# One step of a routing computation moved from slot five to slot six on VectorE, in a linear-attention and mixture-of-experts kernel

## The chip, the cores and the metric

The kernel runs on 1 core of one Trainium2 chip, as one launch. The metric is the device time of the launch in microseconds (us), median of several runs. TensorE's granted clock was 0.999 of full speed in the profiled execution.

## The reference

`x` has 4 sequences of 2048 tokens of 256 numbers. The output is `x + attention(xn) + experts(xn)`, where `xn` is the layer norm of `x` over its last axis.

- Attention: 8 heads with keys of 128 and values of 64. `q`, `k`, `v` are products of `xn` with weights, `alpha = sigmoid((xn @ Wg + bg) / 16)` is a decay for each token and head. A state per head follows `state = alpha * state + k v^T` from token to token, and a token's output is `q` times the state. The outputs are multiplied by `sigmoid(xn @ Wog)` and by `Wo`.
- Experts: `scores = sigmoid(xn @ gate_w^T)` over 64 experts in 8 groups of 8, plus a bias. A group's score is the sum of its two highest entries. The four best groups are kept, and among their experts the eight best. Their scores, brought to a sum of 2.5, are the weights. Each expert takes its tokens in order up to 256, and applies `silu(x w_gate) * (x w_up)` and `w_down`. The results are added to their tokens with the weights.

```python
sfc = scores + gate_bias[None, :]
group_scores = jax.lax.top_k(sfc.reshape(n, G, E // G), 2)[0].sum(-1)
gidx = jax.lax.top_k(group_scores, TG)[1]
```

## The kernel before

**Tiles and steps.** The tokens are cut into 16 tiles, each of 128 tokens of each of the four sequences (512 tokens in all). The attention goes through the tiles in 16 steps, one tile a step, since each needs the state that the one before left. A step has a slot 0 and slots 1 to 8 (`s`), one for each head, and each slot has up to five places (`place`) at which other work is put "beside" the attention (the functions `beside`). The order of every engine's program is written out by hand: an engine works through its instructions in the order of its own `step` function, and waits on semaphores (`wait_ge`) for the others. There is no planner.

**What is beside the attention.** In the early steps (kind "norm", steps 0 to 4) each step normalises and routes three more tiles: first, second and third tile of the step, which are `3c+1`, `3c+2` and `3c+3` for step `c`. Step 5 ("count") and step 6 ("slots") make the lists of the experts' tokens, steps 7 to 14 run eight experts each, and step 15 is the last. On VectorE steps 1 to 3 are a hardware loop, and steps 0 and 4 are written out.

**Routing one tile on VectorE** has five parts, each a chain of small instructions:
- `gates` (L1333) adds the bias to the decay's input; `decays_products` (L1339, L1341, L1344) makes the running products of the decays.
- `route_groups` (L1351 to L1364), thirteen instructions: the biased scores, and for each group the sum of its two highest, into `gsc`. It needs ScalarE's `score` (L1093).
- `route_ranks` (L1372 to L1378): the groups' ranks, from `gsc`.
- `route_top` (L1385 to L1392): the eight best experts.
- `route_weights` (L1401 to L1406): their weights. GpSimd then stores them.

For the second tile of a step: TensorE makes the logits in slot 4 (L723), ScalarE `score` in slot 4, VectorE the group scores at the head of slot 5 and ranks and best experts at the end of slot 6, and the weights in slot 7. `statistics` (L1315 to L1320) and `scales` (L1326, L1327) of the third tile are in slot 6, with ScalarE's square root (L1071) between them and its `normalise` (L1078) behind them.

**The attention on VectorE.** At the start of slot `s` VectorE multiplies the scores of head `s-1`, which TensorE made in bank 2 (L847), by the decays, into `At` (L1533). TensorE's scores of the next head wait until that has read the bank. Then comes a decay scan of a later head (L1512). In odd slots VectorE scales the queries of a pair of heads into `carry` (L1545): ScalarE's copy of the queries in slots 2, 4 and 6 (L1142) of the same step waits for one of those scalings. In even slots TensorE makes the update (L879) and the outputs of the pair (L865, L868), which need both `At` of the pair. VectorE then gates the outputs (`pair_gated`, L1555) and brings the state up (`pair_state`, L1569 and L1572; in step 0 a copy, L1564). ScalarE copies the update (L1156), TensorE transposes it back (L891), and L1572 or L1564 needs that. Then ScalarE's high part of the gated outputs (L1160) and VectorE's low part (L1576, `outs_low`). In slot 8 VectorE also makes the low part of the next tile's tokens (L1416), for which TensorE waits at the start of its next step (L810). Queries and keys are projected at L795.

**VectorE's order in slots 5 and 6** of an early step before the change is: `At`, ends, scan, `route_groups` of the second tile, `decays_products` of the second tile, queries scaled; `At`, `statistics`, scan, `scales`, `pair_gated`, `pair_state`, `route_ranks` and `route_top` of the second tile, `outs_low`.

Of the kernel before, what the change touches and what calls it, by code (L numbers as in the profile page):

```python
# [77 lines left out]
def build(nc, x_in, Wq, Wk, Wv, Wo, Wg, bg, Wog, gate_w, gate_bias, w_gate, w_up, w_down, out):  # L78
    with ExitStack() as ctx:
# [236 lines left out]
        def is_first(c):  # L316
            return isinstance(c, int) and c == 0
# [975 lines left out]
        def _(dve):  # L1293
            tt, ts = dve.tensor_tensor, dve.tensor_scalar

            def chained(semaphore, base):

                n = [0]

                def link(ins, apart=False):  # L1300
                    n[0] += 1
                    ins.then_inc(semaphore, 1)
                    if apart:
                        wait_apart(dve, semaphore, base + n[0])
                    else:
                        dve.wait_ge(semaphore, base + n[0])
                return link, n
# [14 lines left out]
            def scales(c):  # L1322
                link, n = chained(norm_chain, c * NORM_CHAIN + 2)
                dve.wait_ge(std_ready, c + 1)
                wait_past(dve, xn_ready, c)
                link(dve.reciprocal(rstd, std))  # L1326
                dve.scalar_tensor_tensor(shift, mv[:, :, 0], -1.0, rstd, ALU.mult, ALU.mult).then_inc(rstd_ready, 1)  # L1327
# [18 lines left out]
            def route_groups(c):  # L1346

                link, n = chained(route_chain, c * ROUTE_CHAIN)
                dve.wait_ge(score_ready, c + 1)
                sfc_t = sfc.rearrange("p a b -> p (a b)").rearrange("p (b e) -> p b e", b=B)  # L1350
                link(tt(sfc_t, score, bias_e[:, None, :].broadcast_to([P, B, E]), ALU.add))  # L1351

                tt(hi1, sfc[:, :, 0:4], sfc[:, :, 4:8], ALU.max)
                link(tt(lo1, sfc[:, :, 0:4], sfc[:, :, 4:8], ALU.min))
                tt(mid, hi1[:, :, 0:2], hi1[:, :, 2:4], ALU.min)
                tt(hi2, hi1[:, :, 0:2], hi1[:, :, 2:4], ALU.max)
                link(tt(lo2, lo1[:, :, 0:2], lo1[:, :, 2:4], ALU.max))
                link(tt(lo2, lo2, mid, ALU.max))
                tt(mid[:, :, 0:1], hi2[:, :, 0:1], hi2[:, :, 1:2], ALU.min)
                tt(hi3, hi2[:, :, 0:1], hi2[:, :, 1:2], ALU.max)  # L1360
                link(tt(lo3, lo2[:, :, 0:1], lo2[:, :, 1:2], ALU.max))
                link(tt(lo3, lo3, mid[:, :, 0:1], ALU.max))
                gsum = gsc.rearrange("p b g -> p (b g)")
                link(tt(gsum[:, :, None], hi3, lo3, ALU.add), apart=True)  # L1364
                assert n[0] == ROUTE_LINKS[0]

            def route_ranks(c):

                link, n = chained(route_chain, c * ROUTE_CHAIN + sum(ROUTE_LINKS[:1]))
                left_out = rank.rearrange("p (b g) -> p b g", b=B)  # L1370
                for b in range(B):
                    ins = dve.max(top8[:, b, :], gsc[:, b, :])  # L1372
                link(ins, apart=True)
                link(dve.memset(top8[:, :, TG:K], BIG), apart=True)
                for b in range(B):
                    ins = dve.match_replace(left_out[:, b, :], top8[:, b, :], gsc[:, b, :], -TAKEN)
                link(ins)
                link(tt(left_out, left_out, gsc, ALU.is_equal))  # L1378
                assert n[0] == ROUTE_LINKS[1]

            def route_top(c):

                link, n = chained(route_chain, c * ROUTE_CHAIN + sum(ROUTE_LINKS[:2]))
                masked_g = masked.rearrange("p b e -> p (b e)").rearrange("p (a g) -> p a g", g=EG)
                ins = dve.scalar_tensor_tensor(masked_g, rank[:, :, None].broadcast_to([P, B * G, EG]), -BIG, sfc,  # L1385
                                               ALU.mult, ALU.add)
                link(ins, apart=True)
                for b in range(B):
                    ins = dve.max(top8[:, b, :], masked[:, b, :])
                link(ins, apart=True)  # L1390
                for b in range(B):
                    ins = dve.match_replace(left[:, b, :], top8[:, b, :], masked[:, b, :], -TAKEN)  # L1392
                link(ins)
                assert n[0] == ROUTE_LINKS[2]

            def route_weights(c):

                link, n = chained(route_chain, c * ROUTE_CHAIN + sum(ROUTE_LINKS[:3]))
                wait_past(dve, sel_kept, c)
                wait_past(dve, wt_stored, 16 * c)  # L1400
                link(tt(chosen, left, masked, ALU.not_equal))  # L1401
                link(tt(weight, score, chosen, ALU.mult))
                link(dve.tensor_reduce(total, weight, AX.X, ALU.add))
                link(ts(total, total, 1e-20, None, ALU.add))
                link(dve.reciprocal(inv, total))
                dve.scalar_tensor_tensor(weight, weight, SCALE_OUT, inv[:, :, None].broadcast_to([P, B, E]),  # L1406
                                         ALU.mult, ALU.mult).then_inc(weight_ready, 1)
                assert n[0] == ROUTE_LINKS[3]
# [223 lines left out]
            def beside(c, kind, s, place):  # L1632


                if kind == "norm":
                    n = STEP_N * c + 1 + s // 3
                    if s == 0 and place == 3:
                        if not is_first(c):
                            route_groups(n - 1)
                            scales(n)  # L1640
                    if s in (3, 6) and place == 1:
                        scales(n)
                    if (s, place) in ((0, 4), (3, 3), (6, 3)):
                        route_ranks(n - 1)
                        route_top(n - 1)
                    if s % 3 == 1 and place == 1:
                        route_weights(n - 1)
                    if (s, place) in ((1, 3), (4, 3), (H, 1)):
                        gates(n)
                    if s in (2, 5) and place == 0:  # L1650
                        route_groups(n)
                    if (s, place) in ((2, 1), (5, 1), (H, 3)):
                        decays_products(n)
                    if s in (2, H) and place == 3 and not (isinstance(n, int) and n == C - 1):
                        statistics(n + 1)
                if kind == "count" and s == 0 and place == 3:
                    route_groups(C - 1)
                    route_ranks(C - 1)
                if kind == "count" and s == 0 and place == 4:
                    route_top(C - 1)  # L1660
                    route_weights(C - 1)
                if kind == "count" and s > 0:
                    for pe_place in {2: (1, 2), 3: (3,)}.get(place, ()):
                        if (s, pe_place) in COUNT_AT:
                            keep_group(COUNT_AT.index((s, pe_place)))
                    if place == 3 and s == H:
                        keep_totals()
                if kind == "slots" and s == 0 and place == 1:
                    keep_firsts()
                if kind == "slots" and (s, place) in FOUR_AT:  # L1670
                    count_four(FOUR_AT.index((s, place)))
                if kind == "slots" and s == H and place == 3:
                    make_lists()
                if kind == "experts" and s > 0:
                    if place == 0:
                        if s > 1:
                            tokens_low_e(c, s - 1)
                        if s == H:
                            hidden_low(c, s - 2)
                            down_low(c, s - 2)  # L1680
                    if place == 1 and 1 < s < H:
                        expert_out(c, s - 2)
                    if place == 2 and s < H:
                        expert_hidden(c, s - 1)
                        weights_low_e(c, s)
                        if s < H - 1:
                            hidden_low(c, s - 1)
                            down_low(c, s - 1)
                    if place == 4 and s == H:
                        expert_hidden(c, s - 1)  # L1690
                        expert_out(c, s - 2)
# [107 lines left out]
```

## Time and profile before

| what | value |
|---|---|
| median of 3 runs | 1258.42 us (1258.26 to 1258.51) |
| the profiled execution | 1258.32 us, span 1256.7 us |
| TensorE busy over the span | 1233.2 us (98%) |
| VectorE | 976.3 us (78%) |
| ScalarE | 624.1 us (50%) |
| GpSimd | 483.9 us (39%) |
| chain that ended last | PE 83%, DVE 11%, issue 3%, ACT 2%, DMA 1% |

The profile is of one execution. "Busy" is the time in which an engine has an instruction in work, and the chain is followed back from the last instruction to whatever released each. PE is TensorE, PEld its weight loads, DVE VectorE, ACT ScalarE, POOL GpSimd. Times in the timelines are us from the start of the span. The projections of the values that begin the early steps (L810) start at 14.1, 87.5, 162.2, 236.6 and 311.0 us, and those of the step behind them at 384.9.

### The profile page before, as it was taken

The page shows a single profiled execution, that of the slowest core. Times are in us where ns is not written, and L with a number is a line of the kernel's source. Part 1 is how long each engine was busy: PE and PEld are TensorE (multiplying, and loading weights), DVE is VectorE, ACT ScalarE, POOL GpSimd, SP SyncE. Part 2 cuts the span into 40 slices and gives each one's busy share as a digit, 9 for nine tenths or more (in the row PEclk, how much of TensorE's full clock was granted, in tenths as well). Part 3 has the DMA queues.
Part 4 walks back from the last instruction along what each step waited for, and adds up shares of the span by engine and source line. Part 5 has one row for each costly group of instructions (what it writes and reads, how often), then busy time and mean ns, then how long its engine had stood idle before and what let it go on. Part 6 is the DMA issues. An engine that isn't in the chain of part 4 may idle for free.

```text
span 1256.7 us, 28686 instructions
## 1 busy us (share of the span) xinstructions
PE 1233.2 (98%) x9922; PEld 1092.0 (87%) x9922; DVE 976.3 (78%) x2343; ACT 624.1 (50%) x1319; POOL 483.9 (39%) x377
## 2 busy tenths in 40 slices
PE   7899999999999999999999999999999999999998
PEld 6788888888888888899999999998999999989987
DVE  6997878889797579778688587786885877868834
ACT  6675756666574544444444344444443444444432
POOL 2110011001101035238457365484574754745720
PEclk9999999999999999999999999999999999999999
DMA  6576534355342313258487476584875766747765
GB/s 241 169 239 217 179 120 159 123 173 173 117 165 77 102 68 102 86 144 195 108 186 180 124 176 150 139 192 109 196 166 125 169 157 143 188 108 193 170 188 181
DMA packets 124920, 194.68 MB, mean 155 GB/s; under 512 B 12016, under 2 KB 98608, under 8 KB 124592
## 3 DMA queue, kind: packets, MB, share of 16 engines
q1 hardware_dynamic: 94384, 147.99, 36.7%
q0 software_dynamic: 30464, 45.83, 20.0%
q8 instruction: 34, 0.56, 0.2%
q14 instruction: 38, 0.31, 0.1%
HBM read 148.62 MB, written 57.74 MB: 164 GB/s over the span
## 4 chain that ended last, share of the span: by engine, by line
PE 83%; DVE 11%; issue 3%; ACT 2%; DMA 1%; DVEq 0%; SPq 0%; ACTq 0%
PE bank L795 24%; PE bank L939 7%; PE bank L847 7%; PE bank L810 7%; PE bank L907 7%; PE bank L827 6%; PE bank L879 4%; PE bank L865 4%; PE bank L950 4%; PE bank L868 4%; PE bank L838 3%; PE bank L891 2%; PE bank L929 2%; DVE Dt L1512 2%; DVE At L1533 1%
## 5 line engine op out<-in xcount | busy, mean ns | idle before, releaser
L635 POOL DMA_INDIRECT acc<-arena,idx_all x128 | 220.2, 1720 | 146.2 <-DMA acc<-res 53.5
L627 POOL DMA_INDIRECT arena<-table,idx_all x132 | 166.6, 1262 | 157.0 <-ACT share L1166 95.7
L795 PE MATMUL bank<-xp,wq 128*128 128x512 f32 x768 | 209.2, 408 | 0.0
L795 PE MATMUL bank<-xp,wk 128*128 128x512 f32 x768 | 202.1, 398 | 0.0
L795 PEld LDWEIGHTS bank<-xp,wk 128*128 128x128 f32 x768 | 138.5, 188 | 29.0
L795 PEld LDWEIGHTS bank<-xp,wq 128*128 128x128 f32 x768 | 137.0, 190 | 25.2 <-issue 0.5
L1512 DVE TENSOR_TENSOR_SCAN Dt<-decay,eye_b 128x512 f32<-128x512 f32 x128 | 157.4, 1231 | 0.0
L1142 ACT ACTIVATE kT<-bank 128x512 f32<-128x512 f32 x128 | 76.3, 596 | 121.0 <-PE bank L795 120.9
L847 PE MATMUL bank<-qT,kT 128*128 128x128 f32 x1024 | 135.3, 275 | 1.1 <-DVE At L1533 1.1
L847 PEld LDWEIGHTS bank<-qT,kT 128*128 128x128 f32 x1024 | 124.9, 192 | 2.0 <-DVE At L1533 1.3
L1142 ACT ACTIVATE qT<-bank 128x512 f32<-128x512 f32 x128 | 76.6, 598 | 89.3 <-PE bank L795 83.7
L1533 DVE TENSOR_TENSOR At<-bank,Dt 128x512 f32<-128x512 f32 x128 | 87.6, 685 | 27.9 <-PE bank L847 26.3
L601 POOL DMA_DIRECT2D table<-arena x16 | 12.4, 775 | 249.0 <-DVE arena L1406 233.4
L939 PEld LDWEIGHTS bank<-xgT,wgu_p 128*128 128x128 f32 x768 | 99.0, 188 | 6.5 <-issue 1.4
L810 PE MATMUL bank<-wv,xp 128*128 128x512 f32 x384 | 102.3, 401 | 1.1 <-DVE xp L1416 0.7
L865 PE MATMUL bank<-At,V 128*64 128x128 f32 x1024 | 98.7, 273 | 4.7 <-DVE At L1533 4.7
L939 PE MATMUL bank<-xgT,wgu_p 128*128 128x256 f32 x768 | 102.0, 282 | 0.0
L827 PE MATMUL bank<-xp,wog 128*128 128x512 f32 x384 | 101.7, 400 | 0.0
L907 PEld LDWEIGHTS bank<-wo,gT 128*128 128x128 f32 x720 | 93.3, 188 | 5.6
L907 PE MATMUL bank<-wo,gT 128*128 128x256 f32 x720 | 94.7, 280 | 0.0
L868 PE MATMUL bank<-carry,state 128*64 128x128 f32 x960 | 94.2, 273 | 0.0
L1146 ACT ACTIVATE V<-bank 128x512 f32<-128x512 f32 x64 | 38.2, 597 | 93.6 <-PE bank L810 93.5
(176 smaller groups left out, 2314.0 us busy)
## 6 DMA issues: line engine op xcount, KB each, us to landing
decay<-decay_dram SPq DMA_DIRECT2D x64, 512.0 KB, 5.0
carry<-decay_dram SPq DMA_DIRECT2D x60, 512.0 KB, 4.7
arena<-in_L_attn_x_dram SPq DMA_DIRECT2D x16, 512.0 KB, 4.7
table<-arena SPq DMA_DIRECT2D x16, 512.0 KB, 3.4
xT_dram<-arena SPq DMA_DIRECT2D x16, 512.0 KB, 3.0
arena<-in_L_ffn_w_gate_dram SPq DMA_DIRECT2D x64, 128.0 KB
arena<-in_L_ffn_w_up_dram SPq DMA_DIRECT2D x64, 128.0 KB
arena<-in_L_ffn_w_down_dram SPq DMA_DIRECT2D x64, 128.0 KB, 3.0
```

The lines of the kernel that those rows point to most:

```text
L627: pool.indirect_dma_start(out=xg[:, e % 2, j, :], out_offset=None, in_=table[:, :], in_offset=bass.IndirectOffsetOnAxis(ap=idx_all[:, e, j ...
L635: pool.indirect_dma_start(out=acc[:, :], out_offset=bass.IndirectOffsetOnAxis(ap=idx_all[:, e, j:j + 1], axis=0), in_=yb[:, e % 2, j, :], ...
L795: last = mm(to[:, :], w[:, part, k, h * DK:(h + 1) * DK], xp[:, other, k, :], start=(k + i == 0), stop=(k == KD - 1 and i == 2))
L810: last = mm(to[:, :], xp[:, part, k, b * P:(b + 1) * P], wv[:, other, k, :], start=(k + i == 0), stop=(k == KD - 1 and i == 2))
L827: last = mm(to[:, :], wog[:, part, k, j * P:(j + 1) * P], xp[:, other, k, :], start=(k + i == 0), stop=(k == KD - 1 and i == 2))
L847: last = mm(bank[2][:, b * P:(b + 1) * P], kT[:, h % 2, b * P:(b + 1) * P], qT[:, h % 2, b * P:(b + 1) * P], start=True, stop=True)
L865: last = mm(bank[5][u * DV:(u + 1) * DV, b * P:(b + 1) * P], V[:, b, h * DV:(h + 1) * DV], At[:, u, b, :], start=True, stop=is_first(c))
L868: last = mm(bank[5][u * DV:(u + 1) * DV, b * P:(b + 1) * P], state[:, 2 * p + u, b, :], carry[:, p % 2, u, b, :], start=False, stop=True)
L907: last = mm(to, gT[:, part, j, b * P:(b + 1) * P], wo[:, other, j, :], start=(j + i == 0), stop=(j == KO - 1 and i == 2))
L939: last = mm(expert_bank[j % 2][:, m * CAP:(m + 1) * CAP], wgu_p[:, part, m, k * I:(k + 1) * I], xgT[:, other, k * CAP:(k + 1) * CAP], star ...
L1142: f(dst[:, h % 2, :], bank_of(kind, "qk"[which], h)[:, :], ACT.Copy, scale=scale).then_inc(qk_cp, 1)
L1512: dve.tensor_tensor_scan(Dt[:, h, :, :].rearrange("p b t -> p (b t)"), decay[:, (h // 2) % 2, (h % 2) * BP:(h % 2 + 1) * BP], eye_b[:, :, ...
```

## The change

In the early steps VectorE no longer makes the second tile's group scores at place 0 of slot 5 but at place 4 of slot 6, which comes behind `pair_state` and directly ahead of place 3, where `route_ranks` and `route_top` of that tile are. In slot 6 the step's current tile `n` is the third, so `n - 1` is the second. The first tile's stay in slot 2 and the third's in slot 0 of the next step. No instruction is added or left out, and no other engine's program changes.

```diff
--- before.py
+++ after.py
@@ -1647,8 +1647,10 @@
                         route_weights(n - 1)
                     if (s, place) in ((1, 3), (4, 3), (H, 1)):
                         gates(n)
-                    if s in (2, 5) and place == 0:
+                    if s == 2 and place == 0:
                         route_groups(n)
+                    if s == 6 and place == 4:
+                        route_groups(n - 1)
                     if (s, place) in ((2, 1), (5, 1), (H, 3)):
                         decays_products(n)
                     if s in (2, H) and place == 3 and not (isinstance(n, int) and n == C - 1):
```

## Rows read from the trace of the kernel before

**Rows 1.** Windows, each engine's busy us (x instructions), clock, DMA, GB/s.
```profile
100.00:200.00 100.00, 97.76 (x763) 84.72 (x762) 83.85 (x291) 62.50 (x131) 11.12 (x12) 1.00 0.51 161
...
400.00:500.00 100.00, 100.00 (x1013) 86.25 (x1012) 74.11 (x141) 45.34 (x103) 29.66 (x30) 1.00 0.27 89
```
**Rows 2.** TensorE's waits: who waited <- for whom, total us, times, longest.
```profile
PE bank L865 <- DVE At L1533: 4.7, 4, 1.2
...
PE bank L891 <- ACT kw L1156: 2.5, 4, 1.0
```
**Rows 3.** Timeline of VectorE, step 1: start, length, instruction, [idle before <- releaser].
```profile
136.13 0.69 DVE L1576 TENSOR_TENSOR gT<-gated,gT 128x512 fp32r<-128x512 f32 x1 [1.09 <-ACT gT L1160]
...
138.55 0.39 DVE L1351 TENSOR_TENSOR arena<-arena 128x256 f32<-128x256 f32 x1
...
141.33 0.28 DVE L1339 COPY arena<-bank 32x128 f32<-32x128 f32 x1 [0.18 <-DVE arena L1364]
...
143.33 0.68 DVE L1533 TENSOR_TENSOR At<-bank,Dt 128x512 f32<-128x512 f32 x1
...
147.45 0.69 DVE L1555 TENSOR_TENSOR gated<-bank,og 128x512 f32<-128x512 f32 x1
...
158.77 0.68 DVE L1533 TENSOR_TENSOR At<-bank,Dt 128x512 f32<-128x512 f32 x1
```
**Rows 4.** Timeline of TensorE, the same stretch of step 1.
```profile
139.67 1.06 PE L847 MATMUL bank<-qT,kT 128*128 128x128 f32 x8
...
144.36 0.39 PE L865 MATMUL bank<-At,V 128*64 128x128 f32 x4
...
147.28 0.66 PE L891 MATMUL bank<-ident,kw 128*128 128x128 f32 x4 [1.00 <-ACT kw L1156]
...
159.72 0.44 PE L865 MATMUL bank<-At,V 128*64 128x128 f32 x4 [1.22 <-DVE At L1533]
```
**Rows 5.** Timelines of VectorE and TensorE, step 0 and the start of step 1.
```profile
66.61 0.40 DVE L1351 TENSOR_TENSOR arena<-arena 128x256 f32<-128x256 f32 x1
...
69.30 0.28 DVE L1339 COPY arena<-bank 32x128 f32<-32x128 f32 x1
...
74.79 0.69 DVE L1564 COPY state<-bank 128x512 f32<-128x512 f32 x1
...
72.96 1.04 PE L865 MATMUL bank<-At,V 128*64 128x128 f32 x16
...
87.50 1.66 PE L810 MATMUL bank<-wv,xp 128*128 128x512 f32 x6 [0.65 <-DVE xp L1416]
```
**Rows 6.** Timelines, step 1, slots 1 and 2: TensorE's instruction and the VectorE instruction it releases.
```profile
110.22 1.06 PE L847 MATMUL bank<-qT,kT 128*128 128x128 f32 x8
...
115.04 0.39 PE L865 MATMUL bank<-At,V 128*64 128x128 f32 x4
...
111.39 0.69 DVE L1533 TENSOR_TENSOR At<-bank,Dt 128x512 f32<-128x512 f32 x1 [1.19 <-PE bank L847]
...
117.01 0.69 DVE L1555 TENSOR_TENSOR gated<-bank,og 128x512 f32<-128x512 f32 x1 [0.27 <-PE bank L868]
```
**Rows 7.** Timeline of ScalarE, slot 6 of step 1.
```profile
146.64 0.59 ACT L1156 ACTIVATE kw<-bank 128x512 f32<-128x512 f32 x1
```
**Rows 8.** Timelines, slot 6 of steps 2, 3 and 4: outputs begin, gating begins.
```profile
218.99 0.39 PE L865 MATMUL bank<-At,V 128*64 128x128 f32 x4
...
221.66 0.69 DVE L1555 TENSOR_TENSOR gated<-bank,og 128x512 f32<-128x512 f32 x1
...
293.44 0.39 PE L865 MATMUL bank<-At,V 128*64 128x128 f32 x4
...
296.10 0.69 DVE L1555 TENSOR_TENSOR gated<-bank,og 128x512 f32<-128x512 f32 x1
...
367.84 0.39 PE L865 MATMUL bank<-At,V 128*64 128x128 f32 x4
...
370.12 0.69 DVE L1555 TENSOR_TENSOR gated<-bank,og 128x512 f32<-128x512 f32 x1
```

## The prediction

> **What bounds the kernel now.** I read the page's busy shares first, then the windows by stretch, then TensorE's waits, and last the three engines' timelines. The window of 100 to 200 us, which lies inside the early steps, has TensorE busy for 97.76 of 100 us with VectorE at 83.85 [rows 1]. So TensorE bounds the stage, and the stage can gain only the few tenths of a microsecond per step in which TensorE stands still. The list of waits names them: 4.7 us in four waits for VectorE's masked scores (At, L1533) and 2.5 us in four waits for ScalarE's copy of the state update (L1156) [rows 2]. Each kind comes once in each of the steps 1 to 4: the first ahead of the outputs of pair 3 (slot 8), the second ahead of the transposes of the update of pair 2 (slot 6). Busy shares don't tell what matters here: VectorE is at 84% and still holds TensorE up, because it has no idle time at all in one stretch of the step. In step 1 that stretch runs from 136.13 us, where VectorE last waited for another engine (ScalarE's high part, 1.09 us), to the At of slot 8 at 158.77, which TensorE is waiting for: its matmuls start at 159.72 after 1.22 us of idleness [rows 3, 4]. (A 0.18 us gap at 141.33 is VectorE behind its own last instruction.) In this stretch VectorE's order is what sets TensorE's end.
>
> **What the change takes from slot 5.** The thirteen instructions of the group scores run from 138.55 to the start of what follows them at 141.33: 2.78 us [rows 3]. Outside the hardware loop, in step 0, the same block takes 69.30 - 66.61 = 2.69 us [rows 5]. Nothing is added or dropped, no DMA and no wait on another engine moves with it (the router's scores that it reads were ready in slot 4, and its reader, the ranks, comes behind both places). What it is moved past on VectorE: the decay products, the scaling of the queries of pair 2, At of slot 6, the statistics and scales of the third tile, a decay scan, and the gating and state update of pair 2. All of these may start up to 2.78 us earlier in step 1. The ranks behind the new place, the low part of pair 2, At of slots 7 and 8, the second tile's weights and the low part of the next tokens can't start earlier than before unless VectorE fills the time it has won.
>
> **Can VectorE fill it?** Two of the moved-past instructions read what TensorE makes, and TensorE isn't late there, so they don't move by the full amount. I take the delay from TensorE's start to VectorE's start from places where VectorE already waited: At began at 111.39 for scores begun at 110.22, 1.17 us; the gating began at 117.01 for outputs begun at 115.04, 1.97 us [rows 6].
> - At of slot 6 (step 1): VectorE would be there at 143.33 - 2.78 = 140.55; the scores began at 139.67, so it starts at 140.84. 0.29 us idle [rows 3, 4].
> - Gating of pair 2: VectorE would be there at 147.45 - 2.78 + 0.29 = 144.96. The outputs of pair 2 began at 144.36 with no wait in front of them, so the gating starts at 144.36 + 1.97 = 146.33. 1.37 us idle.
> The gating thus gains only 147.45 - 146.33 = 1.12 us, and then the block of 2.78 us stands in front of the ranks: these start 2.78 - 1.12 = 1.66 us later than now. That is the sum of the two new idle times. From the ranks to At of slot 8 VectorE is busy without a gap, so this At is 1.66 us later, at 160.43, and TensorE's outputs of pair 3 start at 161.38 instead of 159.72.
>
> **What TensorE wins on the way.** With the queries scaled earlier, ScalarE's copy of the queries, its square root and its copy of the update (146.64 now, L1156) come earlier, and the 1.00 us wait at 147.28 goes [rows 4, 7]. I price this edit at nothing in the sum: between 147.28 and 159.72 TensorE gets 1.00 us ahead, and then waits that much longer for At. It would be worth 1.00 us only if At were not what it waits for next. What is late next is At of slot 7, which frees the bank for the last scores, and At of slot 8.
>
> **The other steps.** By the same rule (new gating start = start of pair 2's outputs + 1.97, then + the block):
> - step 2: 218.99 + 1.97 = 220.96 against 221.66, 0.70 earlier, so 2.78 - 0.70 = 2.08 us later behind it.
> - step 3: 293.44 + 1.97 = 295.41 against 296.10, 2.09 us.
> - step 4 (outside the loop, block 2.69): 367.84 + 1.97 = 369.81 against 370.12, 2.38 us [rows 8].
> - step 0: the state of pair 2 is a plain copy of a TensorE result here, released by the transposes behind the outputs begun at 72.96. It starts at 74.79 now, hard on the update's transposes, and can't move up. So the whole block counts, 2.69 us. TensorE has no wait in its slot 8, but its next step waits for the low part of the tokens (0.65 us at 87.50), which is the last link of the same VectorE chain; 2.69 us goes through [rows 5]. If the copy could move with the outputs, it would be about 2.5.
> Sum: 2.69 + 1.66 + 2.08 + 2.09 + 2.38 = 10.9 us. Each step starts again with VectorE waiting for TensorE (the rows of 6 are such waits, in slots 1 and 2 of step 1), so that one step's lateness neither adds to the next one's nor is taken back there: both engines are shifted together. Behind the early steps TensorE is busy for 100.00 of 100 us [rows 1], which can't give anything back.
>
> The profiled execution took 1258.32 us with a span of 1256.7; the median of the three runs is 1258.42. The sum is made on the former: 1258.3 + 10.9 = 1269.2 us.
>
> **Bounds of what the trace doesn't show.** No row shows VectorE idle in slot 6, so its length is the unknown. From above it is the whole block in each step, as if nothing moved past it gained anything: 2 x 2.69 + 3 x 2.78 = 13.7 us, 1272.0. From below it is nothing, with the 2.5 us of [rows 2] gained: 1255.9. I take 10.9 because both release times come from measured starts of the same instruction pair, and the 1.12 to 0.31 us that the gating may move up are differences of rows. A release time off by 0.3 us would change the sum by 1.2.
>
> **Rivals.**
> 1. Faster: the block falls into time that VectorE has to spare, and the wait for the copy of the update is gone. Place: slot 6, steps 1 to 4. Price: the four waits of L891, 2.5 us, so 1255.9. It decides if pair 2's outputs end so early that VectorE doesn't stand still, or if At of slot 8 has slack. Against it: these outputs start without any wait now and hence can't come earlier, and TensorE already waits 1.1 to 1.2 us for At four times.
> In the Trainium skill, "Perfetto Trace Analysis", section "Optimization Strategy", the advice is to find the gaps on the engine that binds, see which semaphore each waits on, and make that dependency start sooner. Applied to the gap in slot 6 alone it is this rival, 1255.9; applied to both gaps it goes against the change, since the larger one grows.
> 2. No change: the new idle time only equals the wait that goes away and slot 8 absorbs the rest, 1258.4. For it: VectorE's total work is the same. Against it: the stretch behind the ranks has no gap.
> 3. Slower by less: step 0, where TensorE doesn't wait in slot 8, hides its share, and the release times lie some tenths later than my rows (the records of matmul ends are modelled). 10.9 - 2.7 - 1.2 = 7.0 us, 1265.3.
> 4. Slower by more: nothing moves up, 1272.0 as above; the ScalarE work of slot 6 would have to stay where it is, though the queries that it waits for come earlier.
> 5. The change doesn't do what it says: none that I can see. Place 4 of slot 6 stands behind the state update and directly ahead of place 3, where the ranks are, and the tile number is the same in both.
>
> **How the numbers follow.** My forecast (10 to 12 us slower) 0.66, rival 3 0.17, rival 4 0.07, rival 1 0.05, rival 2 0.05. Range 1264.0 to 1272.5: it leaves out the two cases that aren't slower and little besides. A difference under 0.2% (2.5 us) is taken as none: faster 0.04, same 0.06, slower 0.90. Rival 1, at 2.5 us, sits just at that bound, and so part of its chance counts as same.
>
> **What would show it.** In the changed profile: the waits of TensorE for L1156 at L891 gone; VectorE idle ahead of the gating of slot 6 with TensorE's outputs as the releaser, about 1.4 us per step in steps 1 to 3; TensorE's idle time for At up from 5 to 15 us or so, part of it ahead of the scores (L847) of slot 8; the steps longer by 1.7 to 2.7 us each, and everything behind them of the same length. I am wrong if VectorE shows no idle time in slot 6, or if it shows it and the outputs of pair 3 start no later.

## The result, and the profile after

The changed kernel took 1272.94 us (median of 4 runs, 1271.83 to 1274.67) against 1258.46 us: a ratio of 1.0116, interval 1.0104 to 1.0128. It is 14.5 us slower. I had forecast 1269.2 us in a range of 1264.0 to 1272.5. The direction and the chain of waits held; the result lies above the range, and even above the 13.7 us that I had called the most that the order could cost. (The moved block has twelve instructions, and not thirteen as written ahead of the prediction and in it; its measured length of 2.78 us is not touched by that.)

The profiled execution took 1273.22 us with a span of 1271.6. TensorE's waits, which answer to [rows 2]; columns are total, times, longest:

```profile
PE bank L847 <- DVE At L1533: 12.3, 6, 2.4
...
PE bank L865 <- DVE At L1533: 2.6, 2, 1.3
...
PE bank L731 <- ACT arena L1093: 1.7, 2, 1.1
PE bank L950 <- DVE wde_p L1615: 1.0, 1, 1.0
```

The wait for ScalarE's copy of the update (L1156) is gone. TensorE's idle time for At went from 5.8 to 14.9 us in all, most of it now ahead of the scores (L847), and some of that is step 0's and an early one (1.2 us at 38.00) that the kernel before has as well. Why At is late shows in VectorE's timeline of step 1 (2.47 us are step 0's, so 148.78 here is 146.31 in the time of [rows 3]):

```profile
143.28 0.69 DVE L1533 TENSOR_TENSOR At<-bank,Dt 128x512 f32<-128x512 f32 x1 [0.22 <-PE bank L847]
...
148.78 0.69 DVE L1555 TENSOR_TENSOR gated<-bank,og 128x512 f32<-128x512 f32 x1 [1.41 <-PE bank L868]
...
150.71 0.42 DVE L1351 TENSOR_TENSOR arena<-arena 128x256 f32<-128x256 f32 x1
...
153.44 0.38 DVE L1372 MAX8 arena<-arena 128x8 f32<-128x8 f32 x4
...
162.84 0.68 DVE L1533 TENSOR_TENSOR At<-bank,Dt 128x512 f32<-128x512 f32 x1
```

VectorE stands idle for 0.22 and 1.41 us, with TensorE as the releaser, and only then do the group scores stand between the state update and the ranks. TensorE's side of the same slot 8, with no change in the clock:

```profile
158.53 1.16 PE L847 MATMUL bank<-qT,kT 128*128 128x128 f32 x8 [2.38 <-DVE At L1533]
159.52 1.90 PE L723 MATMUL bank<-arena 128*128 128x72 f32 x16
161.35 1.09 PE L879 MATMUL bank<-kw,V 128*64 128x128 f32 x16
...
163.76 0.44 PE L865 MATMUL bank<-At,V 128*64 128x128 f32 x4 [1.31 <-DVE At L1533]
...
166.18 1.65 PE L810 MATMUL bank<-wv,xp 128*128 128x512 f32 x6
```

Step 2 begins in the same way and goes on differently:

```profile
234.72 1.16 PE L847 MATMUL bank<-qT,kT 128*128 128x128 f32 x8 [2.37 <-DVE At L1533]
235.72 3.15 PE L723 MATMUL bank<-arena 128*128 128x72 f32 x16
238.79 1.98 PE L879 MATMUL bank<-kw,V 128*64 128x128 f32 x16
...
244.10 1.65 PE L810 MATMUL bank<-wv,xp 128*128 128x512 f32 x6
```

The same sixteen router matmuls take 3.15 us instead of 1.90, and the update 1.98 instead of 1.09. The windows give the reason; the third number from the right is the granted clock, as a share of 2.4 GHz:

```profile
160.00:164.00 4.00, 2.69 (x33) 2.40 (x34) 3.83 (x8) 0.60 (x1) 1.92 (x2) 1.00 0.13 33
232.00:236.00 4.00, 1.63 (x15) 1.39 (x14) 3.86 (x16) 3.86 (x7) 0.00 (x0) 1.00 0.71 245
236.00:240.00 4.00, 4.00 (x27) 3.87 (x28) 3.83 (x9) 0.00 (x0) 1.36 (x2) 0.52 0.06 19
240.00:244.00 4.00, 4.00 (x44) 3.83 (x41) 2.74 (x4) 1.05 (x3) 0.76 (x1) 0.63 0.48 146
244.00:248.00 4.00, 4.00 (x21) 3.26 (x19) 3.85 (x10) 2.04 (x4) 0.24 (x1) 1.00 0.43 149
...
392.00:396.00 4.00, 4.00 (x29) 3.87 (x30) 4.00 (x6) 0.15 (x1) 2.13 (x2) 0.50 0.14 33
```

Right behind the 2.4 us wait in steps 2 and 4 the granted clock fell from 2.4 to 1.2 GHz for about 7 us. In steps 1 and 3 it did not. The kernel before has no such stretch in the early steps from step 1 on. It does have one near its start, in step 0, behind a wait of 2.30 us, and these rows were there to be read before the prediction. (Of the five later profiles in which TensorE waits 2.1 to 2.3 us at this place, three have the low clock behind it.)

```profile
18.06 0.37 PE L731 MATMUL bank<-ident,idx_all 128*32 128x128 f32 x1 [2.30 <-ACT arena L1093]
```
```profile
16.00:20.00 4.00, 1.94 (x6) 1.58 (x7) 2.38 (x6) 2.75 (x5) 0.05 (x1) 0.76 1.06 379
20.00:24.00 4.00, 4.00 (x16) 3.22 (x15) 3.86 (x11) 2.35 (x4) 0.54 (x1) 0.82 0.51 146
```

A long wait is not the only thing that can come before a fall. In step 0 of the changed kernel a wait of only 1.20 us is followed by 3.4 us at 1.2 GHz, and the eight score matmuls behind it take 1.97 us instead of 1.16:

```profile
38.00 1.97 PE L847 MATMUL bank<-qT,kT 128*128 128x128 f32 x8 [1.20 <-DVE At L1533]
```

It costs nothing in the end: the kernel with filled waits below has no fall there, and its step 0 is 89.97 us too. Steps from one first value projection (L810 behind L731) to the next, in us:

| step | before | changed | difference | predicted | low clock in slot 8 |
|---|---|---|---|---|---|
| 0 (start of the span to step 1) | 87.50 | 89.97 | 2.47 | 2.69 | no |
| 1 | 74.65 | 76.21 | 1.56 | 1.66 | no |
| 2 | 74.42 | 77.92 | 3.50 | 2.08 | yes |
| 3 | 74.41 | 76.42 | 2.01 | 2.09 | no |
| 4 | 73.92 | 77.91 | 3.99 | 2.38 | yes |
| rest of the span | 871.80 | 873.17 | 1.37 | 0 | |

The differences sum to 14.9 us, the difference of the two spans. Without low clock in slot 8 my terms are within 0.22 us; the excess is in the two steps with it, and 1.37 us behind the early steps.

### The profile page after: what moved, and what is told of

It reads as the page before. It is cut to its first block and busy times, and to the rows that moved or that the text cites. A ratio compares the mean times of both kernels' runs of the same rounds, so it can differ in the third digit from the quotient of the medians.

```text
span 1271.6 us, 28686 instructions
## 1 busy us (share of the span) xinstructions
PE 1242.4 (98%) x9922; PEld 1100.3 (87%) x9922; DVE 977.1 (77%) x2343; ACT 623.9 (49%) x1319; POOL 476.8 (37%) x377
## 5 line engine op out<-in xcount | busy, mean ns | idle before, releaser
L635 POOL DMA_INDIRECT acc<-arena,idx_all x128 | 215.8, 1686 | 154.9 <-issue 55.5
L627 POOL DMA_INDIRECT arena<-table,idx_all x132 | 164.0, 1242 | 156.7 <-ACT share L1166 95.4
L847 PE MATMUL bank<-qT,kT 128*128 128x128 f32 x1024 | 137.0, 277 | 12.3 <-DVE At L1533 12.3
L847 PEld LDWEIGHTS bank<-qT,kT 128*128 128x128 f32 x1024 | 125.9, 193 | 14.4 <-DVE At L1533 13.8
L810 PE MATMUL bank<-wv,xp 128*128 128x512 f32 x384 | 103.2, 404 | 1.1 <-DVE xp L1416 0.7
```

What stands on the lines that cost most here:

```text
L627: pool.indirect_dma_start(out=xg[:, e % 2, j, :], out_offset=None, in_=table[:, :], in_offset=bass.IndirectOffsetOnAxis(ap=idx_all[:, e, j ...
L635: pool.indirect_dma_start(out=acc[:, :], out_offset=bass.IndirectOffsetOnAxis(ap=idx_all[:, e, j:j + 1], axis=0), in_=yb[:, e % 2, j, :], ...
L810: last = mm(to[:, :], xp[:, part, k, b * P:(b + 1) * P], wv[:, other, k, :], start=(k + i == 0), stop=(k == KD - 1 and i == 2))
L847: last = mm(bank[2][:, b * P:(b + 1) * P], kT[:, h % 2, b * P:(b + 1) * P], qT[:, h % 2, b * P:(b + 1) * P], start=True, stop=True)
```

## The experiments

All were timed in three rounds beside runs of the kernel before on the same chip. In two of the three sets that kernel took 1260.2 and 1261.4 us instead of 1258.4, so I compare ratios and differences within a set.

**The changed kernel again.** No edit.

> The changed kernel again, beside the other three. Before 1258.4; changed 1271.8 to 1274.7 us. Theory A (order and clock): TensorE waits about 2.4 us for the At of slot 7 in each of steps 1 to 4, and after some of these waits its granted clock is at half for some microseconds (two of four such waits in the first profile); the order alone is worth about 10 us, the clock the rest. The number of waits followed by half clock may differ from run to run, and the time with it by about 2 us for each.

Measured: 1275.45 us against 1260.19, ratio 1.0107 (1.0088 to 1.0126). In this profile steps 1, 3 and 4 ran at low clock behind the wait (77.93, 77.91 and 77.91 us) and step 2 did not (76.42). So which steps are hit changes from run to run. One hit makes a step 77.9 - 76.4 = 1.5 us longer. The matmuls themselves lose more: from the last scores to the transposes of the update step 2 of the first profile takes 8.86 us and step 3 takes 7.13, of which 1.31 is the wait ahead of the outputs, so they take 3.0 us more, and half of that is swallowed by waits that a step without a hit has.

**TensorE kept busy in the wait.**

```diff
+                    if kind == "norm" and s == H:
+                        pe.wait_ge(gate_done, at(c, 4, 3))
+                        for _ in range(12 if is_first(c) else 20):
+                            tr(bank[5][:, 0:P], ident[:, :], ident[:, :])
                     if s > 1 and not is_last(c):
                         scores(c, s - 1)
```

> The changed kernel, in which TensorE makes 20 transposes (12 in step 0) of the identity into bank 5 in slot 8 of each early step, just before the last scores, where it now stands idle for 1.6 to 2.4 us. They do nothing for the result. Theory A: the late At is still late, so the steps stay longer by 1.5 to 2.5 us each, but the clock no longer falls in slot 8: 1268.5 us (1267.5 to 1270). Rival (the low clock has nothing to do with the idle time, or the extra 4 us are something else): unchanged, 1272 to 1275.

Measured: 1270.13 us, ratio 1.0071 (1.0054 to 1.0087), beside 1.0107 for the changed kernel: adding 92 useless transposes makes it 5.3 us faster. It stays 9.9 us above the kernel before, where the expected 1268.5 us was 10.1 above. TensorE's timeline of step 1 and the windows of slot 8 of steps 2 and 4:

```profile
156.00 2.35 PE L1018 MATMUL bank<-ident 128*128 128x128 f32 x20
158.51 1.16 PE L847 MATMUL bank<-qT,kT 128*128 128x128 f32 x8 [0.17 <-DVE At L1537]
159.51 1.90 PE L723 MATMUL bank<-arena 128*128 128x72 f32 x16
```
```profile
236.00:240.00 4.00, 2.69 (x32) 2.41 (x33) 3.83 (x9) 0.60 (x1) 1.42 (x2) 1.00 0.11 34
...
392.00:396.00 4.00, 3.29 (x40) 2.91 (x41) 4.00 (x6) 0.72 (x4) 1.53 (x2) 1.00 0.38 122
```

The scores begin no earlier (158.51 against 158.53), so VectorE's lateness is untouched, and the clock stays up in every early step from step 1 on. The steps are 89.97, 76.20, 76.37, 76.40 and 76.31 us, which is 2.47, 1.55, 1.95, 1.99 and 2.39 above the kernel before. That sum, 10.35 us, is the cost of the order alone; I had worked out 10.9. It is not only the one profile: the mean granted clock was 0.990 to 0.993 in all eight runs of the changed kernel, and 0.997 to 0.999 in the four with filled waits.

**Only half of the wait filled**, 10 transposes (4 in step 0) in place of 20.

> The changed kernel with only 10 transposes (4 in step 0) ahead of the last scores, so that TensorE's wait there is cut from 2.4 to about 1.3 us, and the wait of 1.3 us ahead of the outputs stays. Theory A with the length of the single wait deciding: no step at half clock, 10 us above the kernel before. Rival (the total of the idle time in slot 8 decides, or chance): at least one step at half clock in the profile, 11.5 to 15 us above.

Measured: 1268.79 us against 1258.78, ratio 1.0079 (1.0062 to 1.0096), 10.0 us above. TensorE's waits of step 1 and the windows of slot 8 of step 2:

```profile
158.68 1.16 PE L847 MATMUL bank<-qT,kT 128*128 128x128 f32 x8 [1.28 <-DVE At L1537]
...
163.91 0.44 PE L865 MATMUL bank<-At,V 128*64 128x128 f32 x4 [1.31 <-DVE At L1537]
```
```profile
236.00:240.00 4.00, 2.77 (x33) 2.45 (x31) 3.83 (x9) 0.61 (x2) 1.24 (x2) 1.00 0.27 95
```

Two waits of 1.3 us in one slot leave the clock alone, in all four steps of the profile, and the mean granted clock of the four runs was 0.999 to 1.000.

**The second wait filled instead**, in steps 1 to 4: the same loop with 11 transposes ahead of `outputs(c, 3)`, and none ahead of the scores.

> The changed kernel with 11 transposes ahead of the outputs of pair 3 in steps 1 to 4, which fill TensorE's second wait of 1.3 us in slot 8 and leave the first one of 2.4 us. Theory A: the clock still falls behind the first wait in some of the steps, and in these the transposes now cost time: 14 to 18 us above the kernel before. Rival (the total of the two waits decides): no half clock, 10 us above.

Measured: 1277.55 us (1275.92 to 1285.85) against 1258.78, ratio 1.017 (1.0134 to 1.0207), 18.8 us above, a little more than expected. In the profile, that of the fastest of its runs, steps 2, 3 and 4 have a stretch of low clock, of 6.8, 3.4 and 6.8 us, and take 79.37, 77.77 and 79.35 us. With no wait left to swallow the slow matmuls, and the transposes slowed too, a fall of 6.8 us costs about 3 us here instead of 1.5. Step 2:

```profile
232.00:236.00 4.00, 1.63 (x13) 1.39 (x12) 3.86 (x16) 3.83 (x7) 0.00 (x0) 0.96 0.79 258
236.00:240.00 4.00, 4.00 (x24) 3.87 (x25) 3.83 (x9) 0.00 (x0) 1.40 (x2) 0.50 0.03 8
240.00:244.00 4.00, 4.00 (x39) 3.50 (x37) 2.40 (x3) 0.99 (x3) 0.73 (x1) 0.69 0.45 157
```

So the falls in slot 8 come with the first wait of 2.4 us. They need neither the second wait nor the total of the two.

**The same wait made without the change.** To see whether the moved instructions matter in themselves, I delayed At of slot 7 in the kernel before by products that nobody reads, one of 1024 columns (1.22 us), or that and two of 512 (2.3 us in all).

```diff
+                    if kind == "norm" and s == H - 1:
+                        full = wq[:, 0, 0, :]
+                        tt(wgu_p[:, :, :, :].rearrange("p a m n -> p (a m n)"), full, full, ALU.mult)
                     scores_decayed(c, s - 1)
```

> The kernel before (group scores in slot 5), with one idle product of 1024 columns (about 1.2 us) on VectorE at the head of slot 7 of the early steps, ahead of At. It changes no result. Nothing of the change is in it: it only makes At of slots 7 and 8 late by a set time. Theory A: each step is longer by that time, less what TensorE has in hand in step 0: 4 x 1.2 + 1.0, 5 to 6 us above the kernel before; TensorE waits 1.2 us at the scores of slot 8 and the clock stays up. Rival (the low clock of the changed kernel comes from where its instructions stand, not from the wait): the same here, so this run doesn't tell them apart, but the next one does.

> The same with idle products of 2.4 us in all. Theory A: TensorE waits about 2.4 us at the scores of slot 8, each step is 2.2 to 2.4 us longer, 11 to 12 us in all by the order alone, and as in the changed kernel the clock falls to half behind some of the waits: 13 to 18 us above the kernel before, with at least one stretch at half clock in steps 1 to 4. Rival (the wait has nothing to do with the clock): 11 to 12 us above, clock up throughout.

Measured against 1261.37 us: the short delay 1269.38, ratio 1.0058 (1.0038 to 1.0078); the long one 1279.78, ratio 1.0148 (1.0127 to 1.0169). The short one cost 8.0 us, more than the 5 to 6 expected: its steps are 1.2 to 1.6 us longer from step 1 on, and step 0 1.8. In step 1 At of slot 7 comes 1.60 us later after the step's start than in the kernel before: 1.13 us are the product, 0.35 us are a longer gap between the statistics and the scan of slot 6 (0.26 us of it idle, with no releaser in the profile), and 0.11 us were there before that. Why the gap is there I can't say. It shows no low clock from step 1 on with waits of 0.72 to 0.87 and 1.31 us. The long one, with waits of 1.92 to 2.06 us, does in steps 2, 3 and 4. Its step 2:

```profile
236.04 1.39 PE L847 MATMUL bank<-qT,kT 128*128 128x128 f32 x8 [2.06 <-DVE At L1533]
237.22 3.53 PE L723 MATMUL bank<-arena 128*128 128x72 f32 x16
240.68 1.98 PE L879 MATMUL bank<-kw,V 128*64 128x128 f32 x16
```

So the low clock comes with the long wait, whatever made the wait.

**The group scores at other places.** With VectorE's order as the theory, each place has its own price. Behind the scaling of the queries, at the end of slot 5 (against the kernel before):

```diff
-                    if s in (2, 5) and place == 0:
+                    if (s, place) in ((2, 0), (5, 4)):
                         route_groups(n)
```

> The second tile's group scores at the end of slot 5, behind the decay products and the scaling of the queries, ahead of the At of slot 6. Theory A: VectorE gets no new idle time, At of slots 6, 7 and 8 stand where they were, so the ScalarE wait of slot 6 (L1156 at L891) goes and TensorE waits as much longer in slot 8, about 2.2 us for step 1: 1258.4 us (1257.6 to 1259.2) if the clock holds, up to 1262 if it falls after the longer wait. Rival (the wait in slot 6 is worth its time): 1256.0.

Measured: 1261.21 us against 1260.19, ratio 1.0007 (0.9997 to 1.0017): no change, as expected. In its profile the early steps end at 385.09 us, where those of the kernel before end at 384.90. But the wait at L891 that I said would go is still there, at 1.05 us in step 1. ScalarE's timeline tells why:

```profile
142.21 0.60 ACT L1142 ACTIVATE qT<-bank 128x512 f32<-128x512 f32 x1 [1.02 <-PE bank L795]
142.83 1.28 ACT L1071 ACT_TABLE_LOAD   x1
146.18 0.20 ACT L1071 ACTIVATE arena<-arena 128x4 f32<-128x4 f32 x1 [2.07 <-DVE arena L1320]
146.29 0.58 ACT L1142 ACTIVATE kT<-bank 128x512 f32<-128x512 f32 x1
146.77 0.59 ACT L1156 ACTIVATE kw<-bank 128x512 f32<-128x512 f32 x1
```

The copy of the queries is 1.3 us earlier than in the kernel before, and then the square root waits 2.07 us for the statistics, with the copies behind it. The wait at L891 hangs on the statistics (L1320), which stand behind the group scores in this order too.

At the head of slot 6, ahead of the scales (`if s == 6 and place == 0: route_groups(n - 1)` in the changed kernel):

> The second tile's group scores at the head of slot 6, behind At, statistics and scan, ahead of scales and gating. Theory A: the only new idle time is ahead of At of slot 6, where VectorE waits for the scores: 1.85, 0.3, 0.7, 0.7 and 0.9 us in steps 0 to 4, 4.5 in all, and none ahead of the gating: 1262.9 us (1262 to 1264.5), more if the clock falls. Rival (what costs is any place in slot 6, because the ranks follow directly): near the changed kernel, 1268 or more.

Measured: 1266.86 us, ratio 1.0046 (1.0031 to 1.0061), 6.7 us above in place of 4.5. The waits of TensorE in its profile have a pair that I had not foreseen, 1.2 us in each of steps 1 to 3:

```profile
153.17 0.66 PE L713 MATMUL bank<-ident,arena 128*128 128x128 f32 x4 [0.75 <-ACT arena L1078]
...
155.67 0.66 PE L713 MATMUL bank<-ident,arena 128*128 128x128 f32 x4 [0.46 <-ACT arena L1104]
```

The scales behind the group scores make ScalarE's normalising late, and TensorE transposes the normalised tokens in slot 7. But this pair explains little of the difference, since steps 1 to 4 are 0.56, 1.00, 1.04 and 0.91 us longer than in the kernel before, against 0.3, 0.7, 0.7 and 0.9 expected. Most of it is in step 0, 2.83 instead of 1.85 us, and there 0.80 us lie ahead of the first projection of the values (14.92 instead of 14.12 us), which the move doesn't touch.

Behind the scales and ahead of the gating (`(s, place) in ((2, 0), (6, 2))`):

> The second tile's group scores in slot 6 behind the scales of the third tile and ahead of the gating of pair 2: one place earlier than the change, on the other side of the gating and the state update. Theory A (the cost is VectorE's idle time ahead of the gating): the group scores fill that idle time, what is left is the wait ahead of At of slot 6, 1.85, 0.3, 0.7, 0.7 and 0.9 us, so 4.5 us above the kernel before, with ScalarE's normalising not late as it was at the head of slot 6, and no low clock, as TensorE's waits come in pieces of about 1.2 us. Rival (any place in slot 6 costs what the change costs): 14 us above.

Measured: 1263.55 us against 1258.78, ratio 1.0038 (1.0024 to 1.0052), 4.8 us above as expected. VectorE's gating of step 1 is no longer preceded by a wait for TensorE:

```profile
142.93 0.69 DVE L1533 TENSOR_TENSOR At<-bank,Dt 128x512 f32<-128x512 f32 x1 [0.22 <-PE bank L847]
...
146.94 0.42 DVE L1351 TENSOR_TENSOR arena<-arena 128x256 f32<-128x256 f32 x1
...
149.85 0.69 DVE L1555 TENSOR_TENSOR gated<-bank,og 128x512 f32<-128x512 f32 x1 [0.29 <-DVE arena L1364]
```

One place further than this, past the gating and the state update, is the change. Those few instructions are the difference between 4.8 and 14.5 us (15.3 when the changed kernel was timed again).

**A version that beats both.** At of slot 8 is what the kernel before waits for. I moved the second tile's weights behind it, and slot 8's decay scan to the end of the step.

```diff
-                    if s % 3 == 1 and place == 1:
+                    if (s, place) in ((1, 1), (4, 1), (H, 0)):
                         route_weights(n - 1)
...
-                    scan_ahead(c, s)
+                    scan_last = kind == "norm" and s == H
+                    if not scan_last:
+                        scan_ahead(c, s)
...
                         outs_low(c, s // 2 - 1)
+                    if scan_last:
+                        scan_ahead(c, s)
```

> The kernel before (group scores in slot 5), with the second tile's weights moved on VectorE from slot 7 to behind At of slot 8, and slot 8's decay scan of the early steps moved to the step's end, where VectorE stands idle at the start of the next step. Theory A: At of slot 8, for which TensorE waits 1.1 to 1.2 us in steps 1 to 4, comes 2.1 us earlier, the low part of the tokens about 0.9 us earlier: 4 x 1.2 and 0.65 us in step 0, 5.4 us below the kernel before (4 to 6). Rival (the start of the next step is bound by the same VectorE work, so that the wait only moves there): no change.

Measured: 1254.78 us against 1258.78, ratio 0.9968 (0.9956 to 0.9979), 4.0 us faster, at the lower end of the 4 to 6 expected. The waits in slot 8 are gone, and in its profile steps 1 to 4 take 73.47, 74.09, 74.12 and 72.53 us instead of 74.65, 74.42, 74.41 and 73.92. Step 0 takes 87.45 us instead of 87.50, so its 0.65 us were not won. Steps 2 and 3 win only 0.3 us each, because TensorE waits there at the start, 0.88 and 0.86 us at 174.61 and 248.69:

```profile
L907 PE MATMUL bank<-wo,gT 128*128 128x256 f32 x240 | 31.8, 281 | 1.7 <-DVE res L1595 1.7
```

The releaser is VectorE's sum of the results. It is late behind the third tile's scales, which VectorE begins after 1.92 us of idleness, for which the profile names no releaser (0.64 us in the kernel before):

```profile
173.69 0.18 DVE L1326 RECIPROCAL arena<-arena 128x4 f32<-128x4 f32 x1 [1.92 <-issue]
```

That the moved scan brings this about is likely, but no run here shows it.

## Why the prediction was right in its mechanism and wrong in its size

- **The new idle time of VectorE.** Right. I had worked out 0.29 and 1.37 us for step 1; the trace has 0.22 and 1.41.
- **The steps' lengths by the order alone.** Right: 1.66, 2.08, 2.09 and 2.38 us for steps 1 to 4, measured where the clock stays up 1.55, 1.95, 1.99 and 2.39. For step 0 I said that the copy of the state can't move up; it did by 0.27 us (74.52 against 74.79 in [rows 5]), so 2.47 instead of 2.69.
- **The step that failed** is the sum of 10.9 us, and with it the bound "From above it is the whole block in each step, as if nothing moved past it gained anything". Both take TensorE's work as fixed and add up waiting time. I had the parts of the wait in the text (in step 1 the 1.22 us that was there, 1.66 us of lateness and 1.00 us won in slot 6, 3.9 us in all; measured 2.38 + 1.31 = 3.7) but never asked how long the single wait at L847 would be, 2.4 us, and what such a wait does to the granted clock. The slower clock of the matmuls behind it was a term that I put at nothing without a reason. The kernel before has no such wait from step 1 on: its longest there is 1.22 us [rows 4], and its clock stays up. Its one wait of 2.30 us, in step 0, is followed by low clock. The missing term is 1.5 us for each step that is hit, with 2 of 4 and 3 of 4 hit in the two profiles: 3.0 and 4.5 us. Measured by filling the wait, it was 5.3 us. In the Trainium skill, "TensorE: Matmul & The Clock Gate", section "HAM oscillation — how this bites in real kernels", waits for DMA that recur between groups of matmuls bring TensorE's clock down each time, and the group behind runs slow. The trace agrees in kind, with the router's matmuls at 3.15 instead of 1.90 us behind a wait of 2.37, but here the wait is for VectorE, and only some of the waits are followed by low clock.
- **Why the wait in slot 6 goes.** Right that it goes and that it is worth nothing, wrong in why. I put it down to the queries being scaled earlier. The experiment that leaves the statistics where they were keeps the wait, so it was the square root, waiting for the statistics.
- **"Everything behind them of the same length."** Right, as far as the runs can tell. The first profile has 1.37 us more there, 1.01 us of it in one wait for a low part of an expert's weights at 849.28 us (L950). But this stretch varies with the set, whatever the kernel: it took 871.7 us in each of the four profiles of one set, two of them of the changed kernel with transposes, and 872.4 to 875.1 in the other two sets, against 871.8 in the kernel before.
- **Rivals.** The faster one and that of no change fell with the idle time of VectorE in the first profile. Rival 3 (7 us) took two terms off the sum: step 0's, of which the trace shows 2.47 of 2.69 us, and later release times, which came out as reckoned. Rival 4 has nearly the right time, 1272.0, by luck: the instructions did move up, and the low clock made up for it.

What stays open is which of the four steps are hit. The wait is 2.35 to 2.38 us in all of them, and TensorE's work ahead of it is the same. Open too is why the wait of 1.20 us in step 0 was followed by a fall, and the twelve of 1.27 to 1.31 us in slot 8 of the filled and the half filled kernel weren't; the length of the wait is not the whole rule.

## What to carry to other kernels

In a stretch where the second engine is busy without a gap and the first one waits at its end, it isn't only the sum of the second engine's work that counts but whether its order opens a hole in it. Work that needs nothing belongs ahead of the instructions that will have to wait for the first engine, and not behind them. When a wait of TensorE grows, look at how long the longest single one becomes and not only at the total, since the total was worth 10 us here and the one long wait another 4 to 5. A wait can be tested for this with useless transposes before anything else is rearranged. And look through the whole trace of the kernel before, its start too, for a wait as long as the one that the change will make.

## What the runs showed of the hardware

In slot 8 of steps 1 to 4, single waits of TensorE of 1.92 to 2.38 us were followed by 1.2 GHz in 2 to 3 of 4 cases in each of four profiles, 11 of 16 in all, ten times for 6.8 us and once for 3.4. Waits up to 1.64 us, also two of 1.3 us that began 5.2 us apart, were followed by it in no case in any profile from the end of step 0 on; in step 0 one of 1.20 us was, for 3.4 us. Useless transposes in half of a wait of 2.4 us were enough to keep the clock at 2.4 GHz.
